# Weight loads of the second and third grouped product issued from ScalarE instead of SyncE

## The chip, the cores and the metric

One core of a Trainium2 chip runs the whole kernel. The metric is the device time of one execution in microseconds (us). About 0.5% (8 us here) is what a measurement of this kernel can tell from no change.

## What is computed

The reference is a small transformer-like block on 8 sequences of 256 tokens with 256 features: a cross attention with a state-space filter, a "fast feed-forward" attention, a second cross attention and a mixture of experts, each added to `x`. Only the second part matters here. In it q, k and v of every token come from a hard-routed tree:

```python
node = jnp.zeros(x.shape[:2], dtype=jnp.int32)
for _ in range(DEPTH):                       # DEPTH = 8
    logit = jnp.einsum('bsd,bsd->bs', x, nw[node]) + nb[node]
    node = 2 * node + 1 + (logit > 0).astype(jnp.int32)
leaf = node - NN                             # one of 256 leaves
h = act(jnp.einsum('bsd,bsdl->bsl', x, w1[leaf]) + b1[leaf])
return jnp.einsum('bsl,bsld->bsd', h, w2[leaf]) + b2[leaf]
```

It is done for q, k and v (three sets of trees and leaves, ReLU), then for the result of the attention (a fourth set, GELU).

## The kernel before

`group_products` does q, k and v as three grouped products, f = 0, 1, 2, one after the other. The 2048 tokens are sorted by leaf into 16 tiles of 128 rows (NT = 16), and the 256 leaves form 32 groups of 8 (NG8 = 32). A merge of tiles and groups gives 47 units (UNITS = 47) for one product; a unit is one tile with one group of leaves. Which group and tile a unit takes is read from registers, since it depends on the data. Units are numbered through by `no(f, u)`, so the three products are one stream of 141 units.

The weights of all 32 groups of one product lie in SBUF in `leaf_w1` and `leaf_w2` (named `leaf_w` in the profile), in one copy: 16 pairs of groups (PAIRS8 = 16). The next product's pair j may be loaded only when the current product's unit 2j+16, the last that can use those groups, has been multiplied. `load_pair` (L1424) issues three transfers for a pair: two of 128 KB for `w1` (L1429) and one of 256 KB for `w2` (L1431).

What each engine does for a unit:

- TensorE (PE): `hidden` (L2161, four matmuls into `gq_psH`), then `output` of the unit two earlier (L2171, two matmuls into `gq_psY`). For the first 16 units of a product it also does `turn` (L2147, L2149), which transposes one token tile.
- ScalarE (ACT): `fetch` (L1886) copies the group's weights, at an address from a register, into one of three buffers `gq_w` for the unit two ahead; `activate` (L1894) applies the ReLU to `gq_psH`; for the first 16 units `turned` (L1873) moves a transposed tile to SBUF.
- VectorE (DVE): `leaf_only` (L2047) masks the hidden values, `add` (L2066) adds the output to `gq_y`, `token` (L2038) reads leaf numbers of a token tile.
- GpSimd (POOL): `place` (L1764) scatters tokens into sorted order, `seed` (L1776) gathers the bias rows into `gq_y`.
- SyncE (SP): issues the plain transfers, in an order written out by hand: tiles of tokens (`tile`, L1819, a ring of 6 buffers), weights (`pair`, L1828 to L1831), results (`store`, L1825).

SP's order in product f is: tiles 6 to 15 of f; pairs 0 to 2 of f+1; tiles 0 to 5 of f+1; then the stores of f one by one, each pair of f+1 put in ahead of the store whose unit comes at the time of the pair's last use; then tiles 6 to 15 of f+1, and so on. So the last pair stands ahead of the last store, and both stand ahead of tile 6 of the next product. `pair` waits for the semaphore `y_ps` that TensorE raises at the end of each `output`.

ACT's loop over units n is, in short: `fetch` of unit n+2, `activate` of unit n, and `turned` of a tile where there is one. In the kernel before ACT issues no transfer in this stage.

Of the kernel before, what the change touches and what calls it, by code (L numbers as in the profile page):

```python
# [18 lines left out]
D = 256  # L19
# [1390 lines left out]
class GroupWeights:  # L1410
# [10 lines left out]

    PAIR = 3 * 16

    def load_pair(self, sp, f, pair):  # L1424

        at = (f * PAIRS8 + pair) * P
        rows = self.rows[at:at + P]
        for c in range(DC):
            sp.dma_start(self.w1[:, c, pair * GH:(pair + 1) * GH],  # L1429
                         rows[:, c * GH:(c + 1) * GH]).then_inc(self.pair_in[pair], 16)  # L1430
        sp.dma_start(self.w2[:, pair * 2 * D:(pair + 1) * 2 * D],  # L1431
                     rows[:, W1COLS:W1COLS + 2 * D]).then_inc(self.pair_in[pair], 16)

    def load_biases(self, sp):
        for f in range(4):
# [220 lines left out]
def group_products(core, name, first, nf, leaves, weights, places, rows, beside, gelu=False,  # L1656
# [9 lines left out]
    with ExitStack() as own:  # L1666
# [50 lines left out]
        def no(f, u):  # L1717

            return f * UNITS + u
# [5 lines left out]
        def last_unit(t):  # L1725

            return min(t + NG8 - 1, UNITS - 1)
# [27 lines left out]
        with nc.Block() as block:  # L1755
# [54 lines left out]
            @block.sync  # L1810
            def _(sp):
                def tile(f, t):
                    n = f * NT + t
                    if t == 0:
                        sp.wait_ge(placed[f], 16 * NT)
                    if n >= RING:
                        sp.wait_ge(x_ps, n - RING + 1)
                        sp.wait_ge(token_in, n - RING + 1)
                    sp.dma_start(xs[n % RING][:, 0:width(first + f)],  # L1819
                                 core.sorted_x[first + f][t * P:(t + 1) * P, :]  # L1820
                                 ).then_inc(tile_in[n % RING], 16)

                def store(f, t):
                    sp.wait_ge(y_sb, no(f, last_unit(t)) + 1)
                    sp.dma_start(core.sorted_y[first + f][t * P:(t + 1) * P, :],  # L1825
                                 ys[f % 2][:, t * D:(t + 1) * D]).then_inc(stored[t], 16)

                def pair(f, j):  # L1828

                    sp.wait_ge(y_ps, no(f - 1, min(2 * j + NT + 1, UNITS)))  # L1830
                    weights.load_pair(sp, first + f, j)  # L1831

                if route:
                    route.sync(sp)
                    weights.load_biases(sp)
                    for j in range(PAIRS8):
                        weights.load_pair(sp, first, j)
                    for t in range(RING):
                        tile(0, t)
                for f in range(nf):  # L1840
                    if route:
                        for t in range(RING, NT):
                            tile(f, t)
                    if f + 1 < nf:
                        for j in range(EARLY):
                            pair(f + 1, j)
                        for t in range(RING):
                            tile(f + 1, t)
                        j = EARLY
                        for t in range(NT):  # L1850
                            while j < PAIRS8 and 2 * j + NT + 1 <= last_unit(t) + 1:
                                pair(f + 1, j)
                                j += 1
                            store(f, t)
                        for j in range(j, PAIRS8):
                            pair(f + 1, j)
                if not route:
                    for t in range(NT):
                        sp.wait_ge(tile_in[t], 16)
                    beside.sync_ahead(sp)  # L1860
                for t in range(NT):
                    store(nf - 1, t)
                for t in range(NT):
                    sp.wait_ge(stored[t], 16 * nf)

            @block.scalar
            def _(act):
                def turned(f, t):
                    n = f * NT + t
                    act.wait_ge(x_ps, n + 1)  # L1870
                    if f:
                        act.wait_ge(y_ps, no(f - 1, last_unit(t)) + 1)
                    act.activation(xT[:, :, t * P:(t + 1) * P],  # L1873
                                   psX[n % 2][:, 0:(DC + 1) * P].rearrange("p (c k) -> p c k",
                                                                           k=P), ACT.Copy
                                   ).then_inc(x_sb, 1)

                def fetch(f, u, g):

                    if u < NG8 and u % 2 == 0:  # L1880
                        act.wait_ge(weights.pair_in[u // 2],
                                    weights.PAIR * (pair_base + f + 1))
                    n = no(f, u)
                    if n >= 3:
                        act.wait_ge(h_ps, n - 2)
                    act.activation(w1[n % 3][:], weights.w1[:, :, bass.ds(g * P, P)], ACT.Copy  # L1886
                                   ).then_inc(w_sb, 1)

                def activate(f, u, g):
                    n = no(f, u)  # L1890
                    act.wait_ge(h_ps, n + 1)
                    if n >= 2:
                        act.wait_ge(h_sb, n - 1)
                    act.activation(act_h[n % 2][:], psH[n % 2][:, 0:P],  # L1894
                                   ACT.Gelu if gelu else ACT.Relu,
                                   bias=weights.b1[:, first + f, bass.ds(g, 1)]
                                   ).then_inc(h_act, 1)

                if route:
                    route.act(act)  # L1900
                act.wait_ge(weights.b1_in, 16 * 4)
                found = [read_words(act, 0)]
                groups = [next_group(act, found, 0, 0, 0)]
                groups.append(next_group(act, found, 0, 1, groups[0]))
                fetch(0, 0, groups[0])
                fetch(0, 1, groups[1])
                for t in range(3):
                    turned(0, t)
                order = [(f, u) for f in range(nf) for u in range(UNITS)]
                for n, (f, u) in enumerate(order):  # L1910
                    read_later(act, found, f, u)
                    if n + 2 < len(order):
                        groups.append(next_group(act, found, *order[n + 2], groups[n + 1]))
                        fetch(*order[n + 2], groups[n + 2])
                    activate(f, u, groups[n])
                    if u + 3 < NT:
                        turned(f, u + 3)
                    elif u + 3 >= UNITS and f + 1 < nf:
                        turned(f + 1, u + 3 - UNITS)
# [1669 lines left out]
```

## Time and profile before

| | |
|---|---|
| median of 3 runs | 1561.65 us (1555.81 to 1564.58) |
| the profiled execution | 1556.66 us |
| its span, first to last instruction | 1555.0 us |
| PE busy | 1237.4 us (80%) |
| DVE busy | 878.2 us (56%) |
| ACT busy | 548.8 us (35%) |
| POOL busy | 444.8 us (29%) |
| mean granted TensorE clock | 0.891 of full speed |
| DMA, mean of the span | 62 GB/s |

Times in the rows are us from the start of the span. The three grouped products run from about 557 to 802 us. "SPq" is SP's queue of instructions that issue transfers, with the time that the issue takes, not the transfer. "Idle before <-" names what ended an engine's idle time; "remote" is a wait whose releaser the profile didn't find. "xN" merges N instructions in a row.

### The profile page before, as it was taken

To read this page: it belongs to the slowest core of one execution; us is meant where nothing else is said; L and a number is where in the kernel's file an instruction comes from. 1 tells how busy PE (TensorE), PEld (TensorE's weight loads), DVE (VectorE), ACT (ScalarE), POOL (GpSimd) and SP (SyncE) were. 2 spreads that over 40 slices of the span, in tenths; PEclk is the share of its full clock that TensorE was granted. 3 is DMA by queue.
4 is the path that set the end of the run, shared out by engine and by line. 5 is a ranking of instruction groups with operands and counts; after the bars stand their busy time and mean duration, and the time that the engine had idled before them with its cause. 6 is when DMAs were issued, how large, how long until landed. Compare 5 with 4: busy or idle time off the path is not lost. (4 is left out here: it accounts for less than half of the span.)

```text
span 1555.0 us, 24593 instructions
## 1 busy us (share of the span) xinstructions
PE 1237.4 (80%) x7204; PEld 904.1 (58%) x7204; DVE 878.2 (56%) x2508; ACT 548.8 (35%) x1074; POOL 444.8 (29%) x587
## 2 busy tenths in 40 slices
PE   2187999999957773578765856859999979999998
PEld 1085777777746562466644645646666645555554
DVE  7998988998324542446452453633555533454434
ACT  2124566665312131346542314513434432212120
POOL 2248344544440427131226317231121000000000
PEclk9558999999979987799887977967999989999999
DMA  8000000000006332667433625250010000000000
GB/s 264 0 2 1 1 1 1 1 1 1 1 4 179 113 92 99 200 205 246 140 127 124 189 69 121 74 142 7 9 15 8 2 1 0 14 0 13 0 14 14
DMA packets 90116, 97.06 MB, mean 62 GB/s; under 512 B 20040, under 2 KB 74826, under 8 KB 89996
## 3 DMA queue, kind: packets, MB, share of 16 engines
q1 hardware_dynamic: 77708, 70.32, 14.8%
q0 software_dynamic: 12288, 25.26, 6.3%
q8 instruction: 60, 0.98, 0.3%
q14 instruction: 60, 0.49, 0.1%
HBM read 76.59 MB, written 18.96 MB: 61 GB/s over the span
## 5 line engine op out<-in xcount | busy, mean ns | idle before, releaser
L2161 PE MATMUL gq_psH<-gq_xT,gq_w 128*128 (+1 forms) x564 | 101.6, 307 | 47.5 <-ACT gq_act L1894 32.2
L2161 PEld LDWEIGHTS gq_psH<-gq_xT,gq_w 128*128 128x128 f32 x564 | 82.4, 208 | 73.5 <-issue 68.9
L2834 DVE TENSOR_REDUCE c_max<-c_psA 128x8 f32<-128x2048 f32 x32 | 73.4, 2293 | 55.9 <-PE c_psA L2984 55.9
L3310 ACT ACTIVATE m_silu<-m_psG 128x512 f32<-128x512 f32 x48 | 28.7, 597 | 213.5 <-PE m_psU L3430 213.5
L2171 PE MATMUL gq_psY<-leaf_w,gq_hT 128*128 (+1 forms) x282 | 93.0, 413 | 13.0 <-DVE gq_hT L2047 7.9
L3363 DVE TENSOR_TENSOR m_act<-m_silu,m_psU 128x512 f32<-128x512 f32 x48 | 33.0, 687 | 120.7 <-ACT m_silu L3310 106.0
L2066 DVE TENSOR_TENSOR gq_y<-gq_psY,gq_y 128x256 f32 (+1 forms) x141 | 59.7, 423 | 71.2 <-remote 49.9
L3430 PE MATMUL m_psG<-m_xnT,m_gate 128*128 128x512 f32 x192 | 90.7, 594 | 2.1 <-PEq L193 2.1
L3430 PE MATMUL m_psU<-m_xnT,m_up 128*128 128x512 f32 x192 | 90.2, 592 | 0.0
L1776 POOL DMA_INDIRECT gq_y<-in_group_b,gq_row_leaf x48 | 45.6, 950 | 138.6 <-DVE gq_row_leaf L2038 130.3
L2742 ACT ACTIVATE c_probT<-c_psA 128x2048 f32<-128x2048 f32 x32 | 60.1, 1877 | 63.7 <-PE c_psA L3018 63.7
L2047 DVE SCALAR_TENSOR_TENSOR gq_hT<-gq_xT,unit_leaf,gq_act 128x128 f32<-128x128 f32 x141 | 49.6, 352 | 48.9 <-ACT gq_act L1894 28.0
L1894 ACT ACTIVATE gq_act<-gq_psH,leaf_b 128x128 f32<-128x128 f32 x141 | 51.4, 364 | 71.9 <-remote 43.1
L766 DVE MATCH_REPLACE8 s_product_a_rest<-a_top,s_product_a_rest 128x256 f32<-128x256 f32 x192 | 76.1, 409 | 0.0
L206 POOL TENSOR_SCALAR m_rstd<-m_mean_var 128x4 f32<-128x4 f32 x4 | 0.9, 232 | 240.4 <-DVE m_mean_var L1289 240.4
L3442 PE MATMUL m_psD<-m_down,m_act 128*128 128x256 f32 x256 | 60.9, 381 | 7.1 <-DVE m_acc L3388 7.1
L756 DVE MAX8 a_top<-s_product_a_rest 128x8 f32<-128x256 f32 x192 | 64.9, 411 | 1.6
L3388 DVE SCALAR_TENSOR_TENSOR m_acc<-m_psD,m_weight,m_acc 128x256 f32<-128x256 f32 x128 | 53.1, 478 | 22.3 <-PE m_psD L3442 22.3
L3430 PEld LDWEIGHTS m_psU<-m_xnT,m_up 128*128 128x128 f32 x192 | 36.5, 190 | 45.9 <-issue 45.9
L3442 PEld LDWEIGHTS m_psD<-m_down,m_act 128*128 128x128 f32 x256 | 48.1, 190 | 25.6 <-issue 14.2
L1050 PE MATMUL a_psW<-s_tables_a_work,a_w 128*128 128x256 f32 x256 | 60.8, 393 | 2.7 <-ACT s_tables_a_work L664 2.7
L1886 ACT ACTIVATE gq_w<-leaf_w 128x256 f32 (+1 forms) x141 | 58.3, 414 | 5.1 <-issue 2.7
(533 smaller groups left out, 3016.4 us busy)
## 6 DMA issues: line engine op xcount, KB each, us to landing
leaf_w<-in_group_w SPq DMA_DIRECT2D x128, 128.0 KB
leaf_w<-in_group_w SPq DMA_DIRECT2D x64, 256.0 KB
gq_x<-sorted_x_v SPq DMA_DIRECT2D x16, 130.0 KB
gq_x<-sorted_x_k SPq DMA_DIRECT2D x16, 129.5 KB
gq_x<-sorted_x_q SPq DMA_DIRECT2D x16, 129.0 KB
rows_f<-token_rows SPq DMA_DIRECT2D x8, 257.0 KB
a_w<-in_L_xattn_W SPq DMA_DIRECT2D x2, 1024.0 KB, 13.1
sorted_y_q<-gq_y SPq DMA_DIRECT2D x16, 128.0 KB, 3.8
```

The costliest lines, as they stand in the source:

```text
L756: do.mark(dve.max(top[:, j, 8 * r:8 * r + 8], row_in(r, j)))
L766: last = dve.match_replace(rest[:, j, :], top[:, j, 8 * r:8 * r + 8], row_in(r, j), NEG_TAKEN)
L1050: last = pe.matmul(pW[:, 2 + c // 2 % 2, c % 2, :], w1[:, k, c * P:(c + 1) * P], hT[:, k, :], start=(k == 0), stop=(k == DC - 1))
L1886: act.activation(w1[n % 3][:], weights.w1[:, :, bass.ds(g * P, P)], ACT.Copy).then_inc(w_sb, 1)
L2066: dve.tensor_tensor(here, psY[n % 3][:, 0:D], here, ALU.add).then_inc(y_sb, 1)
L2161: last = pe.matmul(psH[n % 2][:, 0:P], w1[n % 3][:, c, :], xT[:, c, bass.ds(g * -P + u * P, P)], start=(c == 0), stop=(c == DC - 1))
L2171: pe.matmul(psY[n % 3][:, 0:D], hT[n % 2][:], weights.w2[:, bass.ds(g * D, D)], start=True, stop=True).then_inc(y_ps, 1)
L2742: act.activation(probT[c][:], psA[:], ACT.Exp, scale=float(DH1) ** -0.5).then_inc(exps.s, 1)
L2834: dve.tensor_reduce(out[:, :, :, SUM_ROW], psA[:], AX_X, ALU.max).then_inc(maxes.s, 1)
L3388: last = dve.scalar_tensor_tensor(acc[:, t, :], psD[:, t, :], wt[:, t, e:e + 1], acc[:, t, :], ALU.mult, ALU.add)
L3430: last = pe.matmul(o[u % 2][:], w[:, u, c, :], xnT[:, c, :], start=(c == 0), stop=(c == DC - 1))
L3442: last = pe.matmul(psD[:, t, :], act_u[u % 2][:, t * P:(t + 1) * P], down[:, u, :], start=True, stop=True)
```

## The change

`load_pair` takes the queue as an argument. SP's function `pair` and its three places in SP's order are taken out; what is left there is tiles and stores. ScalarE gets `next_pair(n)`, which stands right behind `activate` of unit n. It issues pair j of product f+1 at unit 2j+18 of product f (the last two pairs at units 46 and 48, which is unit 1 of the next product), after a wait for `y_ps`. Each of the 32 pairs (16 for k, 16 for v) keeps its three transfers, its sizes and its semaphore. The first product's weights and those of the fourth set stay on SP.

```diff
-    def load_pair(self, sp, f, pair):
+    def load_pair(self, queue, f, pair):
 ...
-            sp.dma_start(self.w1[:, c, pair * GH:(pair + 1) * GH],
+            queue.dma_start(self.w1[:, c, pair * GH:(pair + 1) * GH],
 ...
-                def pair(f, j):
-
-                    sp.wait_ge(y_ps, no(f - 1, min(2 * j + NT + 1, UNITS)))
-                    weights.load_pair(sp, first + f, j)
 ...
                     if f + 1 < nf:
-                        for j in range(EARLY):
-                            pair(f + 1, j)
                         for t in range(RING):
                             tile(f + 1, t)
-                        j = EARLY
                         for t in range(NT):
-                            while j < PAIRS8 and 2 * j + NT + 1 <= last_unit(t) + 1:
-                                pair(f + 1, j)
-                                j += 1
                             store(f, t)
-                        for j in range(j, PAIRS8):
-                            pair(f + 1, j)
 ...
+                def next_pair(n):
+
+                    for f in range(nf - 1):
+                        for j in range(PAIRS8):
+                            last = no(f, min(2 * j + NT + 1, UNITS))
+                            if n == last + 1:
+                                act.wait_ge(y_ps, last)
+                                weights.load_pair(act, first + f + 1, j)
 ...
                     activate(f, u, groups[n])
+                    next_pair(n)
                     if u + 3 < NT:
                         turned(f, u + 3)
```

## Rows read from the trace of the kernel before

**Rows 1.** Busy time by stretch: stretch, length, PE, PEld, DVE, ACT, POOL, clock, DMA share, GB/s.
```profile
595.00:634.00 39.00, 5.33 (x22) 2.99 (x20) 1.55 (x4) 1.57 (x4) 26.87 (x28) 0.55 0.28 99
634.00:653.00 19.00, 17.68 (x97) 14.42 (x98) 12.96 (x35) 12.79 (x35) 0.00 (x0) 0.84 0.73 221
653.00:668.00 15.00, 12.53 (x60) 10.49 (x60) 7.34 (x24) 6.02 (x18) 3.79 (x4) 0.77 0.89 293
...
705.00:722.00 17.00, 17.00 (x108) 13.42 (x108) 13.80 (x39) 13.37 (x36) 1.62 (x2) 1.00 0.76 237
...
742.00:750.00 8.00, 2.89 (x17) 2.15 (x16) 1.21 (x5) 1.72 (x7) 1.45 (x2) 0.74 0.99 345
```

**Rows 2.** ACT in order of time, 705 to 718 us (first and last of thirteen).
```profile
705.82 0.37 ACT L1894 ACTIVATE gq_act<-gq_psH,leaf_b 128x128 f32<-128x128 f32 x1 [0.17 <-PE gq_psH L2161]
...
717.33 0.37 ACT L1894 ACTIVATE gq_act<-gq_psH,leaf_b 128x128 f32<-128x128 f32 x1 [0.44 <-PE gq_psH L2161]
```

**Rows 3.** ACT in order of time, 655 to 660 us: behind a stall.
```profile
655.32 0.42 ACT L1886 ACTIVATE gq_w<-leaf_w 128x256 f32 x1 [2.16 <-PE gq_psH L2161]
655.64 0.35 ACT L1894 ACTIVATE gq_act<-gq_psH,leaf_b 128x128 f32<-128x128 f32 x1
655.89 0.41 ACT L1886 ACTIVATE gq_w<-leaf_w 128x256 f32 x1
...
656.45 0.41 ACT L1886 ACTIVATE gq_w<-leaf_w 128x256 f32 x1
659.11 0.37 ACT L1894 ACTIVATE gq_act<-gq_psH,leaf_b 128x128 f32<-128x128 f32 x1 [2.25 <-PE gq_psH L2161]
```

**Rows 4.** SP in order of time: issues of two pairs of weights.
```profile
706.14 0.81 SPq L1429 DMA_DIRECT2D leaf_w<-in_group_w  x2
706.99 0.43 SPq L1431 DMA_DIRECT2D leaf_w<-in_group_w  x1
...
717.11 0.91 SPq L1429 DMA_DIRECT2D leaf_w<-in_group_w  x2
718.06 1.49 SPq L1431 DMA_DIRECT2D leaf_w<-in_group_w  x1
```

**Rows 5.** All engines in order of time: ACT in units with a turned tile.
```profile
740.72 0.36 ACT L1894 ACTIVATE gq_act<-gq_psH,leaf_b 128x128 f32<-128x128 f32 x1
...
741.60 0.49 ACT L1873 ACTIVATE gq_xT<-gq_psX 128x384 f32<-128x384 f32 x1 [0.52 <-PE gq_psX L2149]
```

**Rows 6.** What ACT and SP waited for (total, times, longest), and ACT and PE within it.
```profile
ACT gq_act L1894 <- remote: 43.1, 5, 23.0
...
SPq L1429 <- remote: 56.9, 2, 55.8
...
610.31 0.37 ACT L1894 ACTIVATE gq_act<-gq_psH,leaf_b 128x128 f32<-128x128 f32 x1 [11.68 <-remote]
...
634.11 0.37 ACT L1894 ACTIVATE gq_act<-gq_psH,leaf_b 128x128 f32<-128x128 f32 x1 [23.02 <-remote]
...
602.16 1.21 PE L2171 MATMUL gq_psY<-leaf_w,gq_hT 128*128 x2 [3.21 <-DVE gq_hT L2047]
...
635.43 0.81 SPq L1429 DMA_DIRECT2D leaf_w<-in_group_w  x2
```

**Rows 7.** DVE, SP and PE in order of time, 740 to 750 us: second product to third.
```profile
740.14 0.42 DVE L2066 TENSOR_TENSOR gq_y<-gq_psY,gq_y 128x256 f32<-128x256 f32 x1
...
744.44 0.55 SPq L1825 DMA_DIRECT2D sorted_y_k<-gq_y  x1
745.09 5.22 SPq L1819 DMA_DIRECT2D gq_x<-sorted_x_v  x7
...
749.05 0.69 PE L2147 MATMUL gq_psX<-identity,gq_x 128*128 128x128 f32 x2 [5.00 <-DMA gq_x<-sorted_x_v]
```

**Rows 8.** The same engines, 676 to 682 us: first product to second.
```profile
676.49 0.42 DVE L2066 TENSOR_TENSOR gq_y<-gq_psY,gq_y 128x256 f32<-128x256 f32 x1
...
677.95 4.42 SPq L1819 DMA_DIRECT2D gq_x<-sorted_x_k  x7
...
681.47 0.44 PE L2147 MATMUL gq_psX<-identity,gq_x 128*128 128x128 f32 x2 [1.07 <-DMA gq_x<-sorted_x_k]
```

More of the change, by code:

```diff
@@ L1428, in load_pair @@
         for c in range(DC):
-            sp.dma_start(self.w1[:, c, pair * GH:(pair + 1) * GH],
-                         rows[:, c * GH:(c + 1) * GH]).then_inc(self.pair_in[pair], 16)
-        sp.dma_start(self.w2[:, pair * 2 * D:(pair + 1) * 2 * D],
-                     rows[:, W1COLS:W1COLS + 2 * D]).then_inc(self.pair_in[pair], 16)
+            queue.dma_start(self.w1[:, c, pair * GH:(pair + 1) * GH],
+                            rows[:, c * GH:(c + 1) * GH]).then_inc(self.pair_in[pair], 16)
+        queue.dma_start(self.w2[:, pair * 2 * D:(pair + 1) * 2 * D],
+                        rows[:, W1COLS:W1COLS + 2 * D]).then_inc(self.pair_in[pair], 16)
     def load_biases(self, sp):
```

## The prediction, made before the changed kernel ran

> **What bounds the kernel now.** I read the busy time by stretch first, to find which parts of the 245 us of the three grouped products run at their limit and which wait. The table shows three kinds of stretch [rows 1]. From 705 to 722 us PE is busy all the time (17.00 of 17) at the full clock (1.00, that is 2.4 GHz): PE is the bound, and DMA moves 237 GB/s beside it. From 653 to 668 us DMA is at 0.89 and PE has gaps. From 742 to 750 us PE works 2.89 of 8 us. From 595 to 634 us nearly nothing runs but POOL, at a clock of 0.55.
>
> Then the engines in order of time, since the question is how much room ACT has. Thirteen `activate`s stand from 705.82 to 717.33 [rows 2]: twelve units in 11.51 us, 0.96 us for a unit, 1.92 for two. A short idle time before each, ended by PE, shows that ACT follows PE here. How fast can ACT go when everything it needs is there? Behind a stall two `fetch`es are 0.57 and 0.56 us apart with an `activate` between them [rows 3]: 0.57 us is ACT's own pace for a unit, less than the sum of the two durations (0.42 and 0.37), since they overlap. So ACT has 0.39 us of room per unit, 0.79 per two units, and no more.
>
> Last, SP's issues: a pair takes 706.14 to 707.42, 1.28 us, where the queue is free, and 717.11 to 719.55, 2.44 us, at its slowest [rows 4].
>
> **The change part by part.** It takes 32 pairs, 96 issues, from SP, which has time, and puts them into ACT's stream, in order with `fetch` and `activate`. Behind a waiting or issuing ACT stand `turned`, the `fetch` of unit n+3 and `activate` of n+1; PE's `hidden` of n+3 needs both, and DVE's `leaf_only` needs the `activate`. There is no row of an issue on ACT in this stage. I take SP's rows as the nearest, and 1.4 us for a pair: near the free 1.28, with a little for the load that most of SP's 32 pairs show. The ends are 0.98 (three issues at the fastest that one row allows, 0.33 each, below what any pair took on SP) and 2.44.
>
> *Pairs 1 to 12 of each product* fall into units without turned tiles. For two units ACT then needs 2 x 0.57 + 1.4 = 2.54 us where it had 1.92: ACT becomes the bound, +0.6 us a pair. Of the 24 pairs I count two as free: after 659 us the clock is at its lower level (mean 0.77 in the stretch [rows 1]), and a unit takes 1.7 us on PE, more than ACT needs. 22 x 0.6 = +13.2 us. With 0.98 it would be +0.2 a pair (+4.4), with 2.44 it would be +1.66 (+36).
>
> *Pairs 13 to 15 of each product* fall into units with a turned tile. ACT idles 0.52 us in such a unit of about 1.4 us [rows 5], and the work passes from PE to ACT and back within the unit, so that an issue is not spread over several. I take half of 1.4, 0.7 us, six times: +4.2 us (ends 0 and 8.4).
>
> *Pair 0 of each product* is a new wait as well. In the first product it meets the long hold: the output of unit 16, which `y_ps` 17 stands for, is at 602.16, yet SP's wait for it ended at 635.43, while ACT ran single `activate`s at 610.31 and 634.11 [rows 6]. Whatever held SP may hold ACT's `y_ps` wait too; then `activate` of unit 19 comes after 635.4 and the 1.3 us of issue, some 2.5 us later than now. I take +2 there, and +1 for the second product: +3 us (ends 0 and 5). The hold itself, 39 us, lies beside POOL's scatters, which nothing here moves; I leave it as it is.
>
> *SP's order.* The stores are no longer behind pairs, and tile 6 of the next product is no longer behind the last pair. From the second product to the third: the last unit's `add` ends at 740.56, its store is issued at 744.44, tile 6 at 745.09, and PE gets it at 749.05 after 5.00 us without work [rows 7]. Without the pairs the store can go at 740.7 and tile 6 at 741.2, 3.9 us earlier; landing takes 3.9 us now with the pairs ahead in the same queue. That is -3.9 us with an unchanged landing, at most -5.0: I take -4.5. From the first to the second the same tail is short: `add` ends at 676.91, tile 6 is issued at 677.95 and PE waits 1.07 us for it [rows 8]: -0.7 us. Together -5.2 us.
>
> The Trainium skill speaks against a part of that ("DMA: Bandwidth & Descriptors", section "Issuing engines are not separate DMA queues"): transfers started from any engine end on the same 16 DMA engines, and a second issuing engine saves only issue time, "usually small relative to the DMA itself". By it the landing would stay at 3.9 us, and the term would be 0.6 us smaller. The trace disagrees on "small": 1.28 us of issue stand beside 512 KB, which at the 293 GB/s of the busiest long stretch take 1.8 us.
>
> *Pace of the weights.* Now SP issues five pairs back to back as it catches up; ACT would hand out one pair in about 2.5 us. DMA is less full, and the gaps of 653 to 664 us (ACT idle 2.16 and 2.25 us [rows 3], then the lower clock) may shrink: 0 to -6 us, I take -2. The weights themselves are in time either way: pair j is issued at unit 2j+18 and used at unit 2j+47.
>
> Sum: 13.2 + 4.2 + 3 - 5.2 - 2 = +13 us. The profiled execution has a span of 1555.0 us and a time of 1556.66; with +13 it would be 1570. The median of the runs shown is 5 us above that execution, 1561.65, and I put the forecast on it: 1575 us.
>
> **The rivals.**
>
> *ACT has the room (no difference).* If an issue on ACT costs 0.98 us a pair, or overlaps with the `activate` before it, the terms are +4.4, +1.5 and +1, against -5.2 and -2: about 0, 1562 us. For it: 0.79 us of room per pair. Against it: no pair on SP took less than 1.25 us.
>
> *The queues part (faster).* If the issues hide wholly (0) and the tiles (-5.2) and the full relief of the DMA load (-6) come, it is -11 us, 1551 us. For it: PE's wait of 5.00 us, and DMA at 0.99 from 742 to 750 us. Against it: PE is the bound in the long stretches, where nothing can be gained, and ACT's room is smaller than the issue. It decides if a pair costs ACT's stream under 0.8 us.
>
> *Issues that block (much slower).* SP still issues 16 stores in the same time, and under load a single issue took 1.49 us [rows 4]. If a pair takes 2.0 us on ACT, and the new waits for `y_ps` add a little, it is 22 x 1.25 + 6 + 5 - 5 = +33 us, 1595 us. On this the Trainium skill ("Perfetto Trace Analysis", section "DMA Instruction — HWDGE (DVE, Sync)") says that the sequencers share the block that generates descriptors, with a wait for its lock; by that rule ACT would wait for SP's stores. No row before shows two engines issuing plain transfers at once.
>
> That a pair would not be loaded at all is out: 2j+18 (or 46, 48) names a unit that exists for every j of both products.
>
> **How the numbers follow.** Forecast (+5 to +25 us) 0.49, room on ACT 0.26, queues part 0.11, issues that block 0.14. The range leaves out most of the faster case and the upper half of the blocking case: 1557 to 1593 us. The bound of 0.5% is 7.8 us, about what a measurement can tell: slower than 1569.5 takes the blocking case and most of the forecast's (0.60), faster than 1553.8 the queues' case (0.11), the rest 0.29.
>
> **What would show it.** In the changed profile, ACT at units 17 to 43 of the first two products should show a pattern of two units: three issues of 0.4 us, and `activate`s 2.4 to 2.6 us apart per two units, with PE's idle time before `hidden` ended by ACT; from 17 to 43 the second product should take about 7 us more than now. Tile 6 of the third product should be issued within 1 us of the last `add`, and PE's wait of 5.00 us should be under 1.5. The hold of 39 us should be as long as now. The prediction is wrong if ACT's issues don't delay the next `fetch` (ACT's pace stays at 0.96 us a unit), or if the hold or the stalls, which I can't explain, change with the order of the transfers; they are larger than all my terms.

## The result, and the profile after

The changed kernel takes 1562.78 us (median of 20 runs, 1556.9 to 1569.4); the kernel before, run beside it, 1553.66 us (20 runs, 1544.77 to 1564.58). The ratio is 1.0053, with a 95% interval of 1.0033 to 1.0072: slower by about 8 us. The forecast was 1575 us, +13. The direction was right, the size was not: costs of +6.2 us in the sum did not come, the largest cost was smaller, and a gain was half of what was forecast (the section on the prediction has the terms). Besides, 8 us of the 12 by which 1575 is too high are not the change at all: the three runs of the kernel before that the forecast stood on had a median of 1561.65 us, the twenty 1553.66.

The profiled execution of the changed kernel has a span of 1556.6 us (time 1558.27), against 1555.0 before. Two executions differ by several us for other reasons, so I compare the traces inside the three products, from the first unit's `add` to the last one's.

The page of the changed kernel lists the transfers by queue (columns: packets, MB, share of 16 engines). The pairs are on a queue of their own, q10:

```profile
q1 hardware_dynamic: 63884, 53.54, 11.5%
q0 software_dynamic: 12288, 25.26, 6.1%
q10 hardware_dynamic: 13824, 16.78, 3.6%
```

Busy time by stretch in the changed kernel, for the stretches of [rows 1] and one more (columns: stretch, its length, then busy us with instructions for PE, PEld, DVE, ACT, POOL, then the granted clock, the DMA share and GB/s):

```profile
595.00:634.00 39.00, 7.62 (x30) 4.55 (x28) 3.19 (x9) 2.04 (x6) 28.87 (x30) 0.58 0.39 127
634.00:653.00 19.00, 14.02 (x63) 10.83 (x63) 8.15 (x23) 6.66 (x21) 0.00 (x0) 0.69 0.47 142
653.00:668.00 15.00, 10.72 (x58) 7.72 (x56) 6.19 (x17) 6.40 (x20) 0.00 (x0) 0.94 0.71 215
705.00:722.00 17.00, 15.09 (x87) 11.45 (x86) 9.73 (x27) 9.35 (x28) 0.95 (x1) 0.94 0.43 130
742.00:750.00 8.00, 6.94 (x43) 5.22 (x42) 4.78 (x13) 3.71 (x12) 0.00 (x0) 1.00 0.90 293
755.00:763.00 8.00, 5.85 (x34) 4.37 (x33) 2.97 (x11) 3.27 (x10) 2.51 (x3) 0.92 0.88 270
```

From 705 to 722 us PE was busy 17.00 of 17 us with 108 matmuls; now 15.09 with 87. In 634 to 653 us it is 14.02 us with 63 matmuls in place of 17.68 with 97. But these windows don't hold the same units. The changed kernel's first `add` comes 3.1 us later (567.41 in place of 564.30), so the stretch without PE work ends 3.2 us later too, and that alone is most of the second difference. The fair comparison is from unit 64's `add` to unit 78's, 707.2 to 720.8 us before and 714.2 to 731.5 us after:

```profile
707.20:720.80 13.60, 13.60 (x87) 10.60 (x86) 10.89 (x31) 10.51 (x29) 0.73 (x1) 1.00 0.89 274
714.20:731.50 17.30, 14.76 (x85) 10.33 (x84) 10.37 (x30) 8.65 (x28) 0.68 (x1) 1.00 0.70 218
```

The same work takes 17.30 us in place of 13.60, at the full clock in both (1.00), and PE now has gaps. DMA has become less full (0.70 from 0.89), so it is not what slows the units. The start of the third product, 2.89 us of PE work in 742 to 750 us before, now lies at 755 to 763 us and holds 5.85; that window begins 0.1 us behind the last `add` of the second product, the one before 1.4 us.

Why PE has gaps can be read on ACT, in order of time (columns: start, duration, engine, line, operation; ACTq is ACT's own queue of issuing instructions). One pair of units is two `fetch`es, two `activate`s and three issues:

```profile
648.41 0.42 ACT L1873 ACTIVATE gq_w<-leaf_w 128x256 f32 x1 [1.21 <-PE gq_psH L2158]
648.74 0.35 ACT L1890 ACTIVATE gq_act<-gq_psH,leaf_b 128x128 f32<-128x128 f32 x1
648.99 0.41 ACT L1873 ACTIVATE gq_w<-leaf_w 128x256 f32 x1
649.17 0.33 ACTq L1429 DMA_DIRECT2D leaf_w<-in_group_w  x1
649.29 0.36 ACT L1890 ACTIVATE gq_act<-gq_psH,leaf_b 128x128 f32<-128x128 f32 x1
649.53 0.46 ACTq L1429 DMA_DIRECT2D leaf_w<-in_group_w  x1
650.02 0.45 ACTq L1431 DMA_DIRECT2D leaf_w<-in_group_w  x1
650.80 0.42 ACT L1873 ACTIVATE gq_w<-leaf_w 128x256 f32 x1 [1.15 <-PE gq_psH L2158]
...
653.19 0.42 ACT L1873 ACTIVATE gq_w<-leaf_w 128x256 f32 x1 [1.15 <-PE gq_psH L2158]
```

The period is 2.39 us (650.80 to 653.19), where [rows 2] gave 1.92 for two units. ACT sits idle 1.15 us ahead of the next `fetch`, and the profile puts that down to PE. But the two issues of 0.46 and 0.45 us lie in this gap: some 0.8 of the 1.15 us is ACT's own queue issuing, and PE waits for ACT. The list of waits of the three products shows how often (total, times, longest). The first line is of the kernel before, the other two of the changed one. The longest wait in the first two lines, 16.6 and 15.2 us, is "the hold", as I call the 39 us at 595 to 634 us in which nearly nothing but POOL works:

```profile
PE gq_psH L2161 <- ACT gq_act L1894: 32.2, 8, 16.6
...
PE gq_psH L2158 <- ACT gq_act L1890: 34.2, 27, 15.2
ACT gq_w L1873 <- PE gq_psH L2158: 27.8, 21, 2.0
```

PE waits for ACT 27 times in place of 8. Outside the hold that is 19.0 us in place of 15.6.

SP in order of time, last stores and first tiles of the next product, and PE's wait for tile 6:

```profile
658.94 24.61 SPq L1825 DMA_DIRECT2D sorted_y_q<-gq_y  x16
683.65 12.13 SPq L1819 DMA_DIRECT2D gq_x<-sorted_x_k  x10
...
731.97 23.26 SPq L1825 DMA_DIRECT2D sorted_y_k<-gq_y  x16
755.33 11.94 SPq L1819 DMA_DIRECT2D gq_x<-sorted_x_v  x10
```
```profile
688.95 0.44 PE L2144 MATMUL gq_psX<-identity,gq_x 128*128 128x128 f32 x2 [2.14 <-DMA gq_x<-sorted_x_k]
...
760.38 0.44 PE L2144 MATMUL gq_psX<-identity,gq_x 128*128 128x128 f32 x2 [1.92 <-DMA gq_x<-sorted_x_v]
```

The last `add` of the second product runs from 754.46 to 754.88, and tile 6 is issued 0.45 us later, at 755.33. PE's wait fell from 5.00 us [rows 7] to 1.92, but the tile landed 5.0 us after its issue, not 3.9. At the start of the second product PE gets tile 6 5.3 us after its issue (683.65 to 688.95), where it was 3.5 us [rows 8].

Where the time went is best read from when each unit's `add` starts. This table is worked out from the start times of DVE's `add` in the traces: us between the starts of two units (18 to 34 means from unit 18's `add` to unit 34's). The last four columns belong to experiments below.

| units | before | after | difference | tail late (e3) | 1460 us: before (e13) | 1460 us: after (e14) | spread (e17) |
|---|---|---|---|---|---|---|---|
| 0 to 18 | 73.6 | 73.3 | -0.3 | 73.6 | 27.1 | 28.9 | 33.6 |
| 18 to 34 | 16.4 | 21.4 | +4.9 | 16.4 | 15.5 | 22.0 | 20.5 |
| 34 to 46 | 22.1 | 20.7 | -1.4 | 22.2 | 17.6 | 21.9 | 18.9 |
| 46 to 49 (second product starts) | 6.2 | 7.2 | +1.0 | 4.4 | 19.9 | 7.3 | 5.1 |
| 49 to 64 | 24.5 | 24.2 | -0.3 | 24.6 | 21.0 | 20.5 | 26.5 |
| 64 to 78 | 13.6 | 17.3 | +3.7 | 13.6 | 13.6 | 17.7 | 23.4 |
| 78 to 94 | 20.8 | 24.1 | +3.3 | 21.7 | 17.6 | 21.1 | 21.4 |
| 94 to 106 (third product starts) | 27.1 | 23.5 | -3.6 | 21.7 | 25.7 | 21.4 | 21.8 |
| 106 to 139 (no pairs move) | 32.3 | 32.0 | -0.2 | 32.1 | 32.1 | 32.0 | 32.1 |
| sum | 236.7 | 243.8 | +7.1 | 230.4 | 190.2 | 192.5 | 203.2 |

So +12 us in the stretches where pairs are issued (18 to 34 and 64 to 94), -3.6 at the start of the third product, and -1.4 to +1.0 elsewhere: +7.1, beside the 8 us of the timed runs. A single trace does not settle so much in every row. The program of e3 was traced twice where the kernel before takes 1550 us: units 34 to 46 take 22.2 us in one trace and 19.7 in the other, all units to 139 230.4 and 226.2. Units 20 to 34 and 67 to 78 are the steady ones, 13.5 and 10.8 us before (the same within 0.1 us in both traces of e3); they take 17.6 and 13.1 us in the changed kernel. The rows from 34 to 64 and from 78 to 94 are uncertain by 2 us or so (e1 and e7, both with all pairs on SP, take 20.1 and 23.3 us from 78 to 94).

### The profile page after: what moved, and what is told of

Its sections match the earlier page's. It is cut to its first block and busy times, and to the rows that moved or that the text cites. A ratio compares the mean times of both kernels' runs of the same rounds, so it can differ in the third digit from the quotient of the medians.

```text
span 1556.6 us, 24589 instructions
## 1 busy us (share of the span) xinstructions
PE 1248.4 (80%) x7200; PEld 907.5 (58%) x7204; DVE 875.2 (56%) x2508; ACT 544.1 (35%) x1074; POOL 445.5 (29%) x587
```

## Experiments: what the pairs cost on ScalarE

The theory is that of the forecast: ACT's stream pays for the time of the issues. The rivals: the new waits for `y_ps` do it, or the traffic of two queues does.

**The wait alone.** The kernel before, pairs on SP, and ACT only waits for `y_ps` where it would issue a pair.

```diff
+                def next_pair(n):
 ...
+                            if n == last + 1:
+                                act.wait_ge(y_ps, last)
```

> The kernel before, with only the change's new waits: ACT waits for y_ps behind the activate of unit 2j+18, but SP still issues every pair in its old order. Theory A (ACT's issue time is the price): ACT has 0.79 us of room per two units and the wait ends at most about 0.5 us after the activate, so 0 to +1 us against before. Theory B (the wait is the price): most of the changed kernel's +8 us, +5 to +8 us. Theory C (the price is the traffic: two queues at once, weights later): 0.

Measured: 1.0016 (0.9994 to 1.0038), and in the trace no unit is more than 0.9 us late against the first `add` (unit 15, in the hold); unit 139 is 0.2 us late. The wait costs nothing that can be seen.

**Two and four issues per pair** in place of three, the bytes unchanged: both halves of `w1` as one transfer of 256 KB, or `w2` as two of 128 KB.

```diff
+            queue.dma_start(self.w1[:, :, pair * GH:(pair + 1) * GH],
+                            rows[:, 0:DC * GH].rearrange("p (c h) -> p c h", c=DC)
+                            ).then_inc(self.pair_in[pair], 32)
```
```diff
+            for k in range(2):
+                queue.dma_start(self.w2[:, (pair * 2 + k) * D:(pair * 2 + k + 1) * D],
+                                rows[:, W1COLS + k * D:W1COLS + (k + 1) * D]
+                                ).then_inc(self.pair_in[pair], 16)
```

> The changed kernel with two issues per pair on ACT instead of three (the two 128 KB transfers of w1 become one of 256 KB; same bytes, same wait, same place). Theory A: an issue takes ACT 0.35 to 0.45 us, and a pair 2.39 us per two units in the changed kernel; with one issue fewer about 2.0, near PE's 1.92: -8 to -10 us against the changed kernel, so -2 to +1 us against before. Theory B and C: as the changed kernel, about +8 us against before.

> The changed kernel with four issues per pair on ACT (w2's 256 KB as two of 128 KB; same bytes, same wait). Theory A: 0.45 us more in ACT's stream for each of some 26 pairs, +10 to +12 us against the changed kernel, +18 to +20 us against before. Theory B and C: as the changed kernel, +8 us against before.

Measured: two issues 1.0007 (0.9986 to 1.0028), four issues 1.0126 (1.0086 to 1.0167); three, the changed kernel itself, 1.0053 (1.0033 to 1.0072). ACT of the kernel with four issues, in order of time:

```profile
650.65 0.41 ACT L1879 ACTIVATE gq_w<-leaf_w 128x256 f32 x1
650.84 0.33 ACTq L1429 DMA_DIRECT2D leaf_w<-in_group_w  x1
650.96 0.36 ACT L1896 ACTIVATE gq_act<-gq_psH,leaf_b 128x128 f32<-128x128 f32 x1
651.20 0.46 ACTq L1429 DMA_DIRECT2D leaf_w<-in_group_w  x1
651.69 0.94 ACTq L1433 DMA_DIRECT2D leaf_w<-in_group_w  x2
652.95 0.42 ACT L1879 ACTIVATE gq_w<-leaf_w 128x256 f32 x1 [1.63 <-PE gq_psH L2164]
...
653.52 0.41 ACT L1879 ACTIVATE gq_w<-leaf_w 128x256 f32 x1
```

The period is 2.87 us (650.65 to 653.52), 0.48 more than 2.39, and the gap before the `fetch` grew by the same 0.48 (1.15 to 1.63): an issue of 0.46 us costs its full time once ACT is the bound. With two issues the period is 2.03 us in one pair of units and 2.26 in the next:

```profile
647.88 0.42 ACT L1878 ACTIVATE gq_w<-leaf_w 128x256 f32 x1 [1.06 <-PE gq_psY L2173]
...
649.91 0.42 ACT L1878 ACTIVATE gq_w<-leaf_w 128x256 f32 x1 [0.79 <-PE gq_psH L2163]
...
652.17 0.42 ACT L1878 ACTIVATE gq_w<-leaf_w 128x256 f32 x1 [0.93 <-PE gq_psY L2173]
```

The bytes are the same in all three, so the amount of traffic is not the price.

The two-issue form was run once more beside other runs of the kernel before:

> The same program as e2_two_issues (the changed kernel with two issues per pair on ScalarE in place of three), which stood at 1.0007 where the kernel before took 1549 us. By the terms found (ScalarE's stream pays by the issue, the start of the second product gains by the tiles that are no longer behind the pairs): 1.000 again where the kernel before takes 1550 us; where it takes 1460 us, the start of the second product gives more (the changed kernel 0.998 there), so 0.992 to 0.996.

Measured there: 1.0031 (1.0000 to 1.0061). The two intervals of the two-issue form overlap, and by timing alone this form can't be told from three issues. The traces separate them where ACT is the bound: units 18 to 34 take 18.3 and 17.7 us with two issues, 21.4 with three, 24.5 with four and 16.4 before.

## Experiments: what SyncE's order is worth

The theory: the gain at the starts of the products comes from tile 6 no longer standing behind the last pairs, whatever queue these are on.

**The last three pairs on SP behind the next product's tiles.** The kernel before, all pairs on SP; only pairs 13 to 15 move, behind tiles 6 to 15 of the product that uses them.

```diff
+    RING, EARLY, LATE = 6 if nf > 1 else NT, 3, 13
 ...
+                    if route and f:
+                        for j in range(LATE, PAIRS8):
+                            pair(f, j)
 ...
-                        for j in range(j, PAIRS8):
-                            pair(f + 1, j)
```

> The kernel before with all pairs on SP, but pairs 13 to 15 put behind tiles 6 to 15 of the next product, so that the last stores and tile 6 don't stand behind them. Theory A's gain term alone: tile 6 of the third product issued some 3 us earlier, -3 to -4.5 us there and -0.5 to -1 us at the second product, in all -4 to -5 us against before. If the wait for tile 6 is only replaced by the next (token reads, seeds, ring of psX), 0 to -1 us.

Measured: 0.9942 (0.9919 to 0.9965), faster than both kernels. In its trace, SP and DMA around the start of the third product:

```profile
737.33 4.90 SPq L1825 DMA_DIRECT2D sorted_y_k<-gq_y  x7
742.33 9.37 SPq L1819 DMA_DIRECT2D gq_x<-sorted_x_v  x10
751.75 0.90 SPq L1429 DMA_DIRECT2D leaf_w<-in_group_w  x2
```
```profile
742.00:750.00 8.00, 6.51 (x44) 5.20 (x43) 3.40 (x13) 5.00 (x16) 3.78 (x4) 1.00 0.71 199
```

Tile 6 goes at 742.33, PE waits for no tile at all, and units 94 to 106 take 21.7 us where the kernel before took 27.1. In the stretches with pairs it differs from the kernel before by 0.9 us at most (units 78 to 94).

The same program again, beside other runs of the kernel before:

> The kernel before with all pairs on SyncE and pairs 13 to 15 issued behind tiles 6 to 15 of the next product, the same program as the run e3_sp_tail, beside other runs of the kernel before. The question is the size of the gain of the order alone: 0.9942 there, 0.9973 for the form with two issues per pair. If the gain is the 6 us that the start of the third product came earlier in the trace, the ratio is 0.995 to 0.997; if e3_sp_tail was a lucky draw and the gain is nothing, it is 0.999 to 1.001.

> The same program as e3_sp_tail and e10_sp_tail_again (ratios 0.9942 and 0.9947). The gain of the order alone, some 8 us, lies at the starts of the second and the third product, so it should be there whatever the time of the kernel before is: ratio 0.993 to 0.997.

Measured: 0.9947 (0.9919 to 0.9975) and 0.9934 (0.9912 to 0.9957). The gain of some 9 us is there each time.

**Only the last three pairs on ACT**, at the changed kernel's units 44, 46 and 48; the rest on SP as before.

> The kernel before with only pairs 13 to 15 of each product on ACT (at units 44, 46 and 48, as in the change); pairs 0 to 12 stay in SP's order. It measures the issues in units with a turned tile, and the tail of SP's order, apart from pairs 0 to 12. Theory A with the sizes read so far: the issues in turned units cost 0 to 1 us in all, and the tail gives 2 to 4 us, since tile 6 is issued early but lands behind the pairs' bytes (5.0 us in the changed kernel against 3.9 us): -1 to -4 us against before. If the turned units cost what was forecast (+4.2): 0 to +2 us.

Measured: 0.9995 (0.9970 to 1.0019). In the trace the last unit is 4.8 us earlier than before; the timed runs show none of it, and since single traces differ by 4 us the 4.8 us may be the execution's. PE's wait for tile 6 is 1.01 us:

```profile
743.73 0.44 PE L2155 MATMUL gq_psX<-identity,gq_x 128*128 128x128 f32 x2 [1.01 <-DMA gq_x<-sorted_x_v]
```

**The changed kernel with pairs 13 to 15 later**, issued by ACT at units 16, 18 and 20 of the next product.

```diff
-                            if n == last + 1:
+                            at = last + 1 if j < 13 else no(f + 1, 16 + 2 * (j - 13))
+                            if n == at:
```

> The changed kernel, but pairs 13 to 15 are issued by ACT only at units 16, 18 and 20 of the next product, where all its token tiles are loaded. If the pairs' bytes beside tile 6 are what makes it land late (5.0 us in the changed kernel), PE's waits for tiles (2.1 and 1.9 us) go and it gains 3 to 6 us against the changed kernel: +2 to +5 us against before; ACT's price for the three pairs (0.5 us each in plain units) takes up to 3 us of it back. If landing is slow for another reason (two queues): as the changed kernel or up to 3 us slower, +8 to +11 us against before.

Measured: 1.0052 (1.0024 to 1.0079), no better than the changed kernel. The trace shows both halves. At the start of the third product PE waits for no tile; DVE, which reads it first, gets tile 6 2.7 us after its issue at 754.68:

```profile
757.34 0.16 DVE L2036 TENSOR_TENSOR gq_row_leaf<-gq_x,bias_row_offset 128x1 int32<-128x1 f32 x1 [0.48 <-DMA gq_x<-sorted_x_v]
...
754.00:762.00 8.00, 7.64 (x51) 6.24 (x51) 3.94 (x15) 5.08 (x15) 3.99 (x5) 1.00 0.69 196
```

PE works 7.64 of 8 us, in the changed kernel 5.85 of 8. But the three pairs now stand where no tile is turned and ACT has no slack, and there the period of 2.39 us shows again:

```profile
782.05 0.33 ACTq L1429 DMA_DIRECT2D leaf_w<-in_group_w  x1
...
784.44 0.33 ACTq L1429 DMA_DIRECT2D leaf_w<-in_group_w  x1
```

Units 106 to 139, which take 32.3 us before and 32.0 in the changed kernel, take 33.9 here.

**Fewer issues, and more late pairs, on SP.** The e3 kernel with two issues per pair; then the same with pairs 10 to 15 late.

> The kernel with the last three pairs behind the tiles on SP, and two issues per pair on SP instead of three. SP is not on the path while it keeps up; it lagged by up to 4 us at the last stores. If that lag is only issue time: 0 to -2 us against the kernel with the late pairs alone, so -9 to -11 us against before. If nothing waits for SP any more: the same, -8 to -9 us.

> As the one before, with pairs 10 to 15 behind the tiles instead of 13 to 15. The weights are used 6 to 16 units after they are issued there. If the DMA load of the second half of a product (0.85 to 0.99 busy) stalls units, it shrinks: -2 to -5 us against the version with three late pairs. If a pair comes too late, ACT waits for it: slower than that version by 1 to 5 us.

Measured: 0.9973 (0.9949 to 0.9996) and 0.9996 (0.9972 to 1.0021). Fewer issues give nothing more on SP, which has time for them. With six late pairs no gain is left in the timed runs: by unit 94 the trace is 2.4 us later than before, where e7 was 2.5 earlier. But the intervals of e7 and e8 overlap, as do those of e3 and e7, so neither difference is shown by the times.

## Experiments: the hold, and why the size depends on the chip

The forecast left the 39 us without PE work, 595 to 634 us [rows 1, 6], as they are. They are larger than all its terms, so I asked what this hold hangs on.

**The third product's scatters later.** POOL scatters tokens for the second and the third product back to back, 32 of them. Here the 16 of the third product come behind the seeds of the second.

```diff
-                    for f in range(1, nf):
-                        place(f)
+                    place(1)
                     for f in range(1, nf):
                         for t in range(NT):
                             seed(f, t)
+                        if f + 1 < nf:
+                            place(f + 1)
```

> The kernel before, with one change on POOL: the 16 scatters that place the values' rows for the third product come behind the 16 seed transfers of the second product, not directly behind the scatters that place the keys' rows. Nothing of the pairs is moved. It asks what the stretch of 39 us without work on TensorE (595 to 634 us of the kernel before) hangs on, which the prediction left as it is. Theory P (the stretch lasts as long as POOL's scatters run back to back): with 16 in place of 32 it is cut to about half, some 20 us shorter, and part of that comes back behind the seeds; the time falls by 5 to 20 us (ratio 0.987 to 0.997). Rival Q (it is something else that ends at its own time, the scatters only stand beside it): the stretch keeps 37 to 40 us, the time within 3 us (ratio 0.998 to 1.002).

Measured: 1.0019 (0.9987 to 1.0050), no difference. But the hold moved. Busy by stretch in this kernel:

```profile
595.00:616.00 21.00, 5.10 (x24) 3.12 (x22) 2.88 (x8) 1.72 (x6) 13.44 (x14) 0.65 0.27 96
616.00:634.00 18.00, 17.89 (x97) 14.74 (x98) 12.69 (x34) 12.16 (x34) 0.00 (x0) 0.84 0.68 214
...
679.00:699.00 20.00, 5.64 (x18) 3.52 (x18) 1.95 (x5) 2.85 (x9) 15.34 (x16) 0.60 0.31 108
```

Sixteen scatters hold PE for about 20 us, and the other sixteen hold it again at 679 to 699 us, where they now stand. The hold follows the scatters, about 1.2 us for each.

> Both edits of the two runs before it together: the third product's scatters behind the second product's seeds, and pairs 13 to 15 on SyncE behind tiles 6 to 15. If the two gains lie in different stretches they add up: by theory P ratio 0.982 to 0.993; by rival Q the ratio is that of the order alone, 0.994 to 0.997.

Both edits together: 0.9960 (0.9924 to 0.9996), the gain of the order alone.

**The scatters spread out.** The kernel with both edits, in which each scatter also waits for a unit of the product that runs, so that POOL pauses between scatters; SP's tiles 0 to 5 of the next product go behind its pairs 3 to 7.

```diff
+                        if f:
+                            pool.wait_ge(y_ps, no(f - 1, NT - 4 + 5 * t // 4))
                         pool.indirect_dma_start(
                             core.sorted_x[first + f],
```

> The kernel of e11_tail_and_place, in which each of the 32 scatters waits on POOL for a unit of the product that runs: scatter t of the next product not ahead of the end of unit 12 + 5t/4 of this one (0.96 us a unit at full pace, so one in 1.2 us, and POOL waits where the units are late); SyncE issues tiles 0 to 5 of the next product behind pairs 3 to 7 instead of ahead of them. In e9_place_later the stretch without work moved whole with the scatters: 19 us at 596 to 616 us for 16 of them, and as much again behind 679 us. Theory S (the other engines stand still only while the scatters run back to back; a gap lets the chain of one unit through): each scatter then costs its unit at most its own 1.26 us in place of 0.96, the two stretches of about 19 us shrink to 5 to 8 us each, and the ratio is 0.976 to 0.990. Rival T (each scatter costs the others its 1.2 us wherever it stands): nothing is gained by spreading, ratio 0.994 to 0.997 as for e11_tail_and_place. Rival U (the order behind it, the placed rows now come later than the tiles want them, costs more than the gap gives): ratio over 1.000, with waits on DMA for the first tiles of the next product.

> The same program as e12_place_spread. Where the kernel before takes about 1550 us and has the stretch of 39 us: theory S (standing still only while scatters run back to back) ratio 0.970 to 0.985; rival T (each scatter costs its 1.2 us) 0.993 to 0.997. Where the kernel before takes about 1460 us: 0.993 again, the spreading being worth nothing there.

> The same program as e12_place_spread and e15_spread_again, once more, for executions in which the kernel before takes about 1550 us and has the stretch of 39 us. Theory S (the others stand still only while scatters run back to back): ratio 0.970 to 0.985 there. Rival T (each scatter costs them its 1.2 us wherever it stands): 0.993 to 0.997. Where the kernel before takes about 1460 us the run says nothing on this: 0.994 as before.

The first two met chips on which the kernel before itself takes 1460.07 and 1460.76 us, not 1550. There the ratio is 0.9935 (0.9913 to 0.9958) and 0.9944 (0.9925 to 0.9962), what the order alone gives there (0.9934). The third met a chip where the kernel before takes 1550.41 us: 0.9813 (0.9752 to 0.9875), 1518.97 us, 31 us faster. The stretch of the hold in that last kernel:

```profile
595.00:634.00 39.00, 29.60 (x177) 22.46 (x178) 21.96 (x63) 19.71 (x56) 16.53 (x18) 1.00 0.83 254
```

PE works 29.60 of 39 us where it worked 7.62 in the changed kernel. In the table, units 0 to 18 take 33.6 us in place of 73.6; some 10 us of that are given back at units 64 to 78, where the third product's scatters now stand. So the hold needs POOL's scatters back to back: in this kernel at most three come without a pause, pauses of 0.6 to 1.3 us stand between such groups, and the units get through. That the pauses do it is the plain reading but not shown apart from the rest: the edit also ties each scatter to a unit and moves SP's tiles 0 to 5 behind pairs 3 to 7, and no run does one of these alone. The interval comes from four runs of this kernel.

**Two kinds of chip.** The kernel before, unchanged, on a chip where it takes 1460 us:

> The kernel before, unchanged, for its trace beside those of the next runs. In the last run its time was 1460 us in place of 1552 us in the runs ahead of it. Theory H (the 92 us are the stretches in which everything but POOL stands still): where the time is about 1460 us, units 16 to 20 of the first product follow at 1 to 2 us and no stretch like 595 to 634 us is there; where it is about 1550 us, the stretch of 39 us is there. Rival G (the 92 us come from elsewhere in the program): the stretch is there in both.

Its profiled execution took 1459.38 us, with a span of 1457.7. The same 32 scatters, at the same pace, stand at 572 to 613 us:

```profile
574.00:613.00 39.00, 35.30 (x211) 28.05 (x212) 26.74 (x76) 23.84 (x66) 29.55 (x32) 0.96 0.73 247
```

POOL is busy 29.55 us as in the hold, yet PE works 35.30 of 39. There is no hold in this trace: the three products take 190.2 us, not 236.7 (46.5 us less). The stretch ahead of them is 10.4 us shorter (first `add` at 553.91 in place of 564.30) and the one behind them 40.4. Back-to-back scatters are thus a condition of the hold, not its whole cause; what differs between the chips no run here shows, nor what the 40 us behind are. The two chips of 1460 us were each met once, eleven minutes apart. That it is the chip, and not something else of that time, is likely but not shown.

The changed kernel beside it:

> The changed kernel, unchanged, timed beside the same runs of the kernel before. If the terms found (22 pairs at 0.5 us on ScalarE, some -3 us at the starts of the products) don't hang on the stretch, the difference is +6 to +10 us whatever the time of the kernel before is. If the pace of ScalarE matters only because the products start late, it is 0 to +3 us.

Measured: 0.9984 (0.9965 to 1.0002): here the change costs nothing. The terms on ACT are there and larger (units 18 to 46: +10.7 us, 64 to 94: +7.5); units 34 to 46, for one, took 22.1 us before on the other chips and take 17.6 here, so nothing there hides what the pairs cost. But the order of SP gives much more. In the kernel before SP and PE at the start of the second product:

```profile
627.01 0.45 SPq L1825 DMA_DIRECT2D sorted_y_q<-gq_y  x1
627.56 2.60 SPq L1819 DMA_DIRECT2D gq_x<-sorted_x_k  x5
```
```profile
633.05 0.69 PE L2147 MATMUL gq_psX<-identity,gq_x 128*128 128x128 f32 x2 [12.54 <-DMA gq_x<-sorted_x_k]
```

The last unit of the first product is added at 614.17, and tile 6 goes 13.4 us later: SP issues tiles 0 to 5 only at 594.21, when the 16 scatters of the second product are done (593 us), and then has 13 pairs and 16 stores to issue one by one. In the changed kernel ACT has issued them meanwhile, and tile 6 goes 0.9 us after the last `add`:

```profile
629.04 0.44 PE L2144 MATMUL gq_psX<-identity,gq_x 128*128 128x128 f32 x2 [2.18 <-DMA gq_x<-sorted_x_k]
```

Units 46 to 49 take 7.3 us in place of 19.9. On the chips of 1550 us the units are late as well, SP catches up, and this term is +1.0 instead of -12.7. The traces sum to +2.4 us for the products on this chip, the timed runs say -2; a single execution doesn't settle so little.

## Why the prediction was right and wrong, step by step

The mechanism was right: ACT's stream has less room than three issues take, becomes the bound there and lengthens the period. What failed are three terms of the sum. Pairs 13 to 15 (+4.2 us) cost nothing that the traces show. The extra that pair 0 was to pay behind the hold (+2 of its +3) did not come. And the gain of SP's order (-5.2) was -2.6, since tile 6 took longer to land. The largest term, pairs 1 to 12, was right in kind and some 3 us too large.

- **Pairs 1 to 12, +13.2 us: right mechanism, too large.** The stretches that hold them (18 to 34, 34 to 46, 64 to 94) give +4.9, -1.4 and +7.0: +10.5, and pair 0 is in it. The sign named in the prediction, about 7 us more from unit 17 to 43 of the second product, came: units 64 to 90 take 35.1 us in place of 28.6. The period is 2.39 us, forecast 2.54. It is 2 x 0.57 us of ACT's own pace and 1.24 for the pair, not 1.4: the sum of the three issues (0.33, 0.46, 0.45). The excess per pair over 1.92 is 0.47, not 0.62. (Over all 32 pairs, the slow ones with them, the issues took 1.33 us a pair on ACT, 1.41 on SP before.)
- **Pairs 13 to 15 in turned units, +4.2 us: wrong.** They are issued beside units 44 to 49 and 91 to 96. Units 44 to 47 take 4.08 us in place of 4.91, units 91 to 94 4.08 in place of 4.11. The step "the work passes from PE to ACT and back within the unit, so that an issue is not spread over several" failed: the issues at 680.02 to 681.32 us lie beside `turned`, `fetch` and `activate` (679.59 to 680.64), and the idle time there was room for them. e5, which moves only these pairs, shows 4.12 and 4.08 us for the same units, and e10, with all pairs on SP, 4.11 and 4.11.
- **Pair 0, +3 us: wrong in its reason.** +2 of it were for the hold, and that extra did not come: units 0 to 18 took 0.3 us less than before. The wait behind the hold, 22.34 us in the changed kernel, replaces one of 23.02 us [rows 6], and e1, which adds only the waits, is not slower beyond its interval. What pair 0 does cost is its issues, like any other pair, and that lies in the +10.5 above: units 17 to 20 take 5.7 us in place of 4.5, units 64 to 67 4.2 in place of 2.9, with issues of pair 1 among them, so that no figure for pair 0 alone can be given.
- **SyncE's order, -5.2 us: too large.** Tile 6 went within 0.5 us of the last `add`, as forecast, but its landing took 5.0 us in place of 3.9 (5.3 in place of 3.5 at the second product). PE's wait of 1.92 us misses the sign "under 1.5". The chosen value counted on a shorter landing; it became longer where the pairs' bytes move at the same time from another queue. Together the two starts gave -2.6 us (+1.0 and -3.6).
- **Pace of the weights, -2 us:** inside the -1.4 of units 34 to 46, not separable, and less than two traces of one program differ by there.
- **The hold: the forecast said "as long as now", and it was.** What was wrong is to leave it unexamined: the chips with and without it give different results for this change (1.0053 and 0.9984).
- **The base:** 8 us of the miss are the median of three runs.

On the landing the Trainium skill ("DMA: Bandwidth & Descriptors", section "Issuing engines are not separate DMA queues") says that transfers from any issuing engine end on the same 16 DMA engines. The runs agree: 5.0 us with the pairs on ACT's queue beside the tile, 2.7 us in e6 and no wait in e3, where no pair moves then. The unchanged 3.9 us that the prediction drew from it did not hold. The same section of the Trainium skill calls the issue time that a second engine saves "usually small"; here 1.24 us of it on an engine with 0.79 us of room is the main loss.

The rival "issues that block" is out: in the steady stretch the issues took 0.33, 0.46 and 0.45 us, no more than on SP, and the longest single one 1.46 us, where SP's longest was 1.49. The rival "ACT has the room" did not come for three issues; the form with two comes nearest to it, where the period is 2.03 to 2.26 us and the excess 0.1 to 0.3.

## What to carry to other kernels

An engine's idle time is room for issues only up to its size per period: three issues of 0.33 to 0.46 us don't fit into 0.79 us, and an idle time that the profile puts down to another engine may be the engine's own issuing. The order gave more than the queue: moving three late pairs behind the tiles that are needed first gives 0.5 to 0.6% on the chips of 1550 us (e3, e10) and 0.7% on one of 1460 us (e16), with nothing on ACT. Where all engines but one stand still, look at what that one issues back to back before tuning anything inside the stretch, and time the kernel on more than one chip.

## What the hardware showed that I had not expected

- POOL's indirect transfers issued back to back (0.96 us each, 0.30 apart) kept PE, ACT and DVE nearly idle for some 1.2 us each, 39 us in all, in every trace of a kernel that issues them so on the chips where the kernel before takes 1550 us, and not on the chip of 1460 us. In the kernel with pauses of about 1 us between groups of them, 40 of the 73.6 us of units 0 to 18 went away. The cause was not found.
- The same program takes 1550 us on three chips of the experiments and 1460 us on two others. Ratios of one chip don't carry over: the changed kernel stood at 1.0053 and at 0.9984.
- An issue of ACT overlaps with the `activate` that stands ahead of it in the program (issue 649.17 to 649.50, `activate` 649.29 to 649.65), but the next `fetch` comes only after the last issue: 0.33 us after its end at 650.47, at 650.80.
